# Quantised codes as smallest fp16 steps, scaled maxima on one engine, and a start without a barrier

## The reference

```python
def _fq(x, delta, zp, n_bits):
    xi = _round_ste(x / delta) + zp
    xq = jnp.clip(xi, 0.0, 2.0 ** n_bits - 1.0)
    return (xq - zp) * delta
...
sim = jnp.einsum('bhid,bhjd->bhij', _fq(q, dq, 128.0, 8), _fq(k, dk, 128.0, 8)) * SCALE
attn = jax.nn.softmax(sim, axis=-1)
out = jnp.einsum('bhij,bhjd->bhid', _fq(attn, dw, 0.0, 8), _fq(v, dv, 128.0, 8))
```

## Time and profile before

| | us |
|---|---|
| median of three runs (1578.14, 1579.74, 1579.89) | 1579.74 |
| the profiled execution | 1576.92 |
| its span in the trace | 1575.1 |
| VectorE busy | 1098.1 |
| PE busy | 1092.8 |
| ScalarE busy | 894.2 |
| GpSimd busy | 681.1 |

### The profile page before, as it was taken

The page is one execution under the profiler, slowest core; times in us unless marked ns, Lnnn a source line. Parts: engine busy times, 40 slices in busy tenths (PEclk is TensorE's granted clock), DMA queues, the critical chain, the costliest instruction groups (busy, mean ns, idle before and its releaser), DMA issues.

```text
span 1575.1 us, 28607 instructions
## 1 busy us (share of the span) xinstructions
PE 1092.8 (69%) x9344; PEld 593.3 (38%) x9344; DVE 1098.1 (70%) x3102; ACT 894.2 (57%) x2546; POOL 681.1 (43%) x1055
## 2 busy tenths in 40 slices
PE   2888888887788797855353545444358778888888
PEld 1333344444333286831120212222225435453545
DVE  2687777777688653678888999877765666666522
ACT  1555554555554464567676797988852344646531
POOL 3321011011011416558888888877741344445310
PEclk9899999999999998975555555555569799999989
DMA  5213142101331112267555576665530121201000
GB/s 184 61 53 92 51 129 75 54 24 50 99 106 49 42 39 82 57 160 122 99 104 109 106 130 115 121 109 106 109 57 14 27 48 35 49 21 43 1 0 27
DMA packets 265219, 116.53 MB, mean 74 GB/s; under 512 B 216936, under 2 KB 253936, under 8 KB 262896
## 3 DMA queue, kind: packets, MB, share of 16 engines
q1 hardware_dynamic: 260112, 108.29, 30.8%
q0 software_dynamic: 2048, 4.20, 0.9%
q10 hardware_dynamic: 2912, 2.22, 0.5%
HBM read 38.80 MB, written 16.45 MB: 35 GB/s over the span
## 4 chain that ended last, share of the span: by engine, by line
PE 35%; POOL 21%; DVE 18%; issue 14%; ACT 9%; DMA 1%; SPq 0%; POOLq 0%; another core or an unknown queue 0%; ACTq 0%; DVEq 0%
POOL arena L2289 12%; ACT arena L1581 4%; PE acc L1199 3%; POOL inv_total L2278 2%; PE trans L1171 2%; DVE minus_top L1980 2%; PE misc L1021 2%; PE misc L1027 2%; PE trans L1323 2%; ACT arena L1528 2%; PE score L1335 2%; PE score L1337 2%; PE trans L1177 1%; POOL arena L2235 1%; PE acc L1385 1%
## 5 line engine op out<-in xcount | busy, mean ns | idle before, releaser
L2289 POOL TENSOR_SCALAR arena<-arena,inv_total 128x512 f16<-128x512 f32 (+1 forms) x512 | 299.7, 585 | 57.3 <-DVE inv_total L2058 16.8
L1980 DVE TENSOR_REDUCE minus_top<-score 128x4 f32<-128x616 f32 (+4 forms) x256 | 200.6, 802 | 95.3 <-PE score L1141 36.9
L2154 POOL TENSOR_TENSOR rstd<-spread,minus_half 128x4 f32<-128x4 f32 x36 | 37.5, 1043 | 489.5 <-DVE spread L1662 414.0
L1581 ACT ACTIVATE arena<-score,minus_top,exp_scale 128x512 f32<-128x512 f32 (+1 forms) x340 | 210.4, 625 | 20.9 <-POOL arena L2289 11.9
L1528 ACT ACTIVATE arena<-trans 128x512 f32<-128x512 f32 x240 | 134.4, 596 | 109.3 <-PE trans L1177 104.0
L1619 ACT ACTIVATE arena<-arena,minus_top 128x154 f32<-128x154 f32 x256 | 105.2, 412 | 129.3 <-DVE minus_top L2123 129.1
L1280 PE MATMUL score<-arena 32*128 32x512 bf16 (+1 forms) x340 | 68.9, 458 | 139.7 <-ACT arena L1581 138.7
L2064 DVE TENSOR_REDUCE top_score<-score 128x2 f32<-128x1024 f32 (+1 forms) x128 | 135.7, 1061 | 0.6 <-PE score L1280 0.5
L2309 POOL TENSOR_TENSOR arena<-arena,inv_total 128x512 f32<-128x512 f32 x64 | 66.5, 1040 | 143.9 <-DVE inv_total L2131 130.0
L1581 ACT ACTIVATE arena<-trans,minus_top,exp_scale 128x154 f32<-128x154 f32 (+1 forms) x172 | 105.5, 620 | 19.2 <-POOL arena L2289 14.9
L2118 DVE CUSTOM_DVE_ANT_0 arena<-score,arena 128x154 f32<-128x154 f32 x256 | 65.9, 313 | 60.6 <-PE score L1360 60.2
(11 more groups left out here) (283 smaller groups left out, 2814.4 us busy)
## 6 DMA issues: line engine op xcount, KB each, us to landing
arena<-q_terms SPq DMA_DIRECT2D x88, 128.0 KB, 2.8
late<-arena SPq DMA_DIRECT2D x128, 64.0 KB, 2.0
q_terms<-arena SPq DMA_DIRECT2D x36, 128.0 KB
late<-k_terms SPq DMA_DIRECT2D x32, 128.0 KB, 3.1
arena<-arena SPq DMA_TRANSPOSE x192, 3.1
by_expert<-zeros SPq DMA_DIRECT2D x2, 1472.0 KB, 9.8
arena<-by_expert SPq DMA_DIRECT2D x10, 256.0 KB
from_expert<-arena SPq DMA_DIRECT2D x10, 256.0 KB
```

The costliest lines, as they stand in the source:

```text
L1581: ins = nc.scalar.activation(probs[:, i % 3, j, of], quant_score[i % 3][:, j, of], ACT.Exp, bias=minus_top[:, at_col:at_col + 1], scale=ex ...
L1980: nc.vector.tensor_reduce(dst, src, axis=AX.X, op=ALU.max, negate=True).then_inc(top_ready, 1)
L2289: ins = nc.gpsimd.tensor_scalar(codes[:, (i - 1) % CODE_SOURCES, j, to], probs[:, (i - 1) % 3, j, of], inv_total[:, at_col:at_col + 1], HA ...
```

## The change

- The codes are written as multiples of the smallest step of fp16, 2 ** -24: GpSimd multiplies by the reciprocal, which now has the step in it, and takes the minimum with 255 steps; the write itself rounds. The transposition goes straight to `pT_codes`, now fp16, the values are fp16 too, and the outputs are scaled by 2 ** 24 at L2072. `copy_codes` and its semaphore go; PE waits for the transposition.
- The maxima are scaled on VectorE, right behind the reduction, with a wait between the two; ScalarE's L1572 goes.
- VectorE's items in the quantised loop are taken from slot i - 1 at step i. The other engines' stay.
- The barrier behind the first loads goes. Loads, memsets and constants stand at the head of the engines' lists, and what needs them waits on new semaphores (`ident_in`, `first_weights_in`, `pads_in`, `pool_set`, `dve_set`). The first weights are the second load on SP; the eight late loads come after unit 0's reads. ScalarE copies one element early, which loads its table. Of the first eight reads of queries, ScalarE's queue issues four. The addition of a bias row to x of sequences 0 and 1 becomes an item "base" at slot 1.

The diff, cut to its core (moved memsets and the new waits inside items left out):

```diff
@@ -13,7 +13,7 @@
 ROUND = 1.5 * 2.0 ** 23
-HALF_ROUND = 1024.0
+CODE_STEP = 2.0 ** -24
 LOWEST = -1.0e30
@@ -21,7 +21,7 @@
 CODE_SOURCES = 4
-QUANT_LAG, WEIGH_LAG, GROUPED_LAG = 6, 8, 2
+WEIGH_LAG, GROUPED_LAG = 8, 2
 
@@ -217,7 +217,7 @@
                 at(exact, f, ("ctx", nxt))
-                at(exact, f + 1, ("x", nxt), ("pads", nxt))
+                at(exact, f + 1, ("x", nxt), ("pads", nxt), ("base", 0), ("base", 1))
             elif u + 1 < B:
@@ -554,13 +555,11 @@
 
-        v_quant, v_quant_tail = put([P, 2, TILES, HEADS, 32], bf16), put([P, 2, HEADS, 32], bf16)
+        v_quant, v_quant_tail = put([P, 2, TILES, HEADS, 32], fp16), put([P, 2, HEADS, 32], fp16)
         probs = put([P, 3, 2, TOKENS])
-        pT_at = quant_at[0]
-        pT_codes = put([P, CODE_SLOTS, 2 * TILES, P], bf16)
-        put = place(arena, [pT_at])
-        pT_raised = put([P, CODE_SLOTS, 2 * TILES, P], fp16)
+        pT_codes = put([P, CODE_SLOTS, 2 * TILES, P], fp16)
         put = place(arena, [0])
+
         codes = put([P, CODE_SOURCES, 2, TOKENS], fp16)
@@ -714,87 +717,27 @@
-        FIRST_SEQUENCE_LOADS, REST_LOADS = 4, 2
-
-        with nc.Block() as once:
-            loads = [(ident[:, :], io["ident"]), (sizes[:, :], io["sizes"].partition_broadcast(P)), (cols[:, :], io["cols"]),
-                     (term_row[:, :], io["term_row"]),
-                     (attn_w[:, 0:4, :], io["attn_w"][:, 0:4, :])]
-            late_loads = [(rows[:, :, :], io["rows"].partition_broadcast(P)), (norm_sel, io["norm_sel"]),
-                          (attn_w[:, 4:20, :], io["attn_w"][:, 4:20, :]), (expert_no[:, :], io["expert_no"]), (masks_f, io["masks"]),
...
+        FIRST_SEQUENCE_LOADS, PAD_LOADS, REST_LOADS = 2, 2, 2
+
+        loads = [(sizes[:, :], io["sizes"].partition_broadcast(P)), (cols[:, :], io["cols"]),
+                 (term_row[:, :], io["term_row"])]
...
+        POOL_SETS, DVE_SETS = 12, 27
+
+        with nc.Block() as block:
+
+            @block.sync
             def _(sp):
+                sp.dma_start(ident[:, :], io["ident"]).then_inc(ident_in, 16)
+                sp.dma_start(attn_w[:, 0:4, :], io["attn_w"][:, 0:4, :]).then_inc(first_weights_in, 16)
                 for dst, src in loads:
                     sp.dma_start(dst, src).then_inc(weights_in, 16)
-                for dst, src in late_loads:
-                    sp.dma_start(dst, src).then_inc(late_in, 16)
-
-            @once.scalar
-            def _(act):
-                for b, loaded in ((slice(0, 1), first_seq_in), (slice(1, B), rest_in)):
-                    act.dma_start(ctx_in[:, b, :, :], io["ctx"][:, b, :, :]).then_inc(loaded, 16)
-                    act.dma_start(x[:, b, :, :], x_dram[:, b, :, :]).then_inc(loaded, 16)
-                    if loaded is first_seq_in:
-                        act.dma_start(pad_rep.rearrange("p b k -> p (b k)"),
-                                      io["mask_BxS2_ff1"].rearrange("b k -> (b k)").partition_broadcast(P))\
-                            .then_inc(loaded, 16)
-                        act.dma_start(pad_col, io["pad_cols"]).then_inc(loaded, 16)
-
-            @once.gpsimd
-            def _(pool):
-                nc.gpsimd.memset(ones, 0.0).then_inc(cleared, 1)
-                nc.gpsimd.memset(ones_tail, 0.0).then_inc(cleared, 1)
-                nc.gpsimd.memset(ones_pad, 0.0).then_inc(cleared, 1)
-                nc.gpsimd.memset(v_tail, 0.0).then_inc(cleared, 1)
-                nc.gpsimd.memset(v_cols, 0.0).then_inc(v_cols_cleared, 1)
-                nc.gpsimd.memset(parts["k"][:, :, CTX:P + 32], 0.0)
-                nc.gpsimd.memset(ctxT_tail4[:, :, :, :], 0.0)
-                nc.gpsimd.memset(k_tail.rearrange("p a g k -> p (a g k)").bitcast(fp32), 0.0)
-                nc.gpsimd.memset(top_cols.rearrange("p a t j c -> p (a t j c)").bitcast(fp32), 0.0)
-                nc.gpsimd.memset(pad_rows, 0.0)
-                nc.gpsimd.memset(zeros[:, :], 0.0)
-                nc.gpsimd.memset(ones_bf[:, :], 1.0)
-                nc.gpsimd.memset(picked[:, :, :].rearrange("p t e -> p (t e)"), 0.0)
-                for i in range(2):
-                    nc.gpsimd.memset(blocks_to[i][:, 0:EXPERTS], 0.0)
-                pool.wait_ge(v_cols_cleared, 1)
-                wide = v_cols.rearrange("p t (a i j) c -> p (t a) i j c", i=2, j=4)
-                for i in range(2):
-                    nc.gpsimd.memset(wide[:, :, i, :, 16 + HD * i:16 + HD * (i + 1)], 1.0)
-
-            @once.vector
-            def _(dve):
-                dve.wait_ge(cleared, 4)
-                for j in range(4):
-                    at_row = 32 * top_place(j)
-                    nc.vector.memset(ones[at_row:at_row + 3, j, :], 1.0)
-                    nc.vector.memset(ones_tail[at_row:at_row + 3, 32 * j:32 * j + CTX_TAIL], 1.0)
-                for s in range(2):
-                    nc.vector.memset(ones_pad[s * STACK:s * STACK + 3, :], 1.0)
-                for j in range(4):
-                    rows_j = slice(32 * j, 32 * j + CTX_TAIL)
-                    for i in range(2):
-                        at_col = i * (P + HD) + 32 * j + 16
-                        nc.vector.memset(v_tail[rows_j, :, at_col:at_col + HD], 1.0)
-                nc.vector.memset(minus_half[:, :], -0.5)
-                dve.wait_ge(weights_in, 16 * len(loads))
-                nc.vector.tensor_copy(ident_bf[:, :], ident[:, :])
-                nc.vector.reciprocal(inv_sizes[:, :], sizes[:, :])
-                for n, name in enumerate(["L1_xattn_sa_bq", "L1_xattn_ca_bq"]):
-                    nc.vector.tensor_scalar(q_bias[:, n:n + 1], col(name), float(HD) ** -0.5, None, ALU.mult)
-                for n in range(2):
-                    q, k, vv, w = (sizes[:, 4 * n + i:4 * n + i + 1] for i in range(4))
-                    nc.vector.tensor_scalar(exp_scale[:, n:n + 1], q, k, float(HD) ** -0.5, ALU.mult, ALU.mult)
-                    nc.vector.tensor_scalar(out_scale[:, n:n + 1], vv, w, None, ALU.mult)
-        with nc.Block() as block:
-
-            @block.sync
-            def _(sp):
                 for u in EXACT_UNITS:
                     width = P + 32 if is_cross(u) else TOKENS
                     keys = (k_stack_ctx if is_cross(u) else k_stack)[:, u % 2, :, :]
@@ -834,9 +777,12 @@
-                        read_queries(slice(0, 2), q_first)
+                        read_queries(slice(0, 2), q_first, slice(0, PRODUCTS // 2))
                     read_queries(slice(0 if u else 2, PAIRS), q_stacked)
                     if u == 0:
+
+                        for dst, src in late_loads:
+                            sp.dma_start(dst, src).then_inc(late_in, 16)
@@ -923,7 +869,7 @@
-                    sp.dma_start_transpose(pT_raised[:, i % CODE_SLOTS, :, :],
+                    sp.dma_start_transpose(pT_codes[:, i % CODE_SLOTS, :, :],
@@ -1285,7 +1236,8 @@
-                    pe.wait_ge(codes_copied, 2 * n + 2)
+                    for i in (2 * n, 2 * n + 1):
+                        pe.wait_ge(codes_turned[i % CODE_SLOTS], 16 * (i // CODE_SLOTS + 1))
@@ -1342,7 +1294,6 @@
-                pe.wait_ge(codes_copied, len(QUANT_STEPS))
@@ -1506,11 +1459,25 @@
+                act.dma_start(ctx_in[:, 0:1, :, :], io["ctx"][:, 0:1, :, :]).then_inc(first_seq_in, 16)
+                act.dma_start(x[:, 0:1, :, :], x_dram[:, 0:1, :, :]).then_inc(first_seq_in, 16)
+                act.dma_start(pad_rep.rearrange("p b k -> p (b k)"),
+                              io["mask_BxS2_ff1"].rearrange("b k -> (b k)").partition_broadcast(P)).then_inc(pads_in, 16)
+                act.dma_start(pad_col, io["pad_cols"]).then_inc(pads_in, 16)
+
+                act.wait_ge(first_use_set, 1)
+                nc.scalar.copy(first_use[:, 1:2], first_use[:, 0:1])
+                act.dma_start(ctx_in[:, 1:B, :, :], io["ctx"][:, 1:B, :, :]).then_inc(rest_in, 16)
+                act.dma_start(x[:, 1:B, :, :], x_dram[:, 1:B, :, :]).then_inc(rest_in, 16)
                 for it in BEFORE[0]:
                     item(*it)
                 act.wait_ge(k_out, 48)
                 for n, term in enumerate(K_TERMS):
                     act.dma_start(k_stack_ctx[n::PRODUCTS, 0, :, :], k_terms_ctx.ap()[:, term, :, :]).then_inc(k_stacked, 16)
+                act.wait_ge(q_out, 48)
+                for n in range(PRODUCTS // 2, PRODUCTS):
+                    act.dma_start(q_stack[n::PRODUCTS, 0, 0:2, :], scratch["q"].ap()[:, Q_TERMS[n], 0:2, :]).then_inc(q_first, 16)
+                act.wait_ge(dve_set, DVE_SETS)
@@ -1569,11 +1536,8 @@
-                    nc.scalar.activation(of_step(minus_top, i), of_step(top_score, i), ACT.Copy,
-                                         scale=exp_scale[:, of:of + 1]).then_inc(quant_top_scaled, 1)
                     if i >= 3:
                         act.wait_ge(codes_ready, i - 2)
-                    act.wait_ge(quant_top_scaled, i + 1)
@@ -1993,6 +1959,31 @@
+                dve.wait_ge(cleared, 4)
+                for j in range(4):
...
```

(39 more changed lines are left out.)

78 lines of the change are left out of this document (67 added, 11 removed).

## The result

The changed kernel takes 1911.66 us (four runs, 1908.42 to 1913.85) against 1578.94 us before (four runs): a ratio of 1.2126, 95% interval 1.2100 to 1.2151. It is a fifth slower, and the prediction (1551, range 1534 to 1574) is wrong in size and in sign. The profiled execution took 1911.02 us, its span 1909.2.

What follows compares the result with a forecast made beforehand. GpSimd was taken to pace self attention 94 per cent of the time, and ScalarE, with GpSimd close behind, cross attention; savings of 7 + 10 + 10 + 0.4 = 27.4 us gave 1551 us, range 1534 to 1574.

Steps and rivals of the forecast that it cites:

- add becomes min: GpSimd's code instruction: add becoming min, and a second operation in the small multiplication, both cost nothing.
- Rival 4: GpSimd's code writes: numbers of a few smallest fp16 steps write slower, 54 ns each decides; far end 1684 us; chance 0.07.
- start, up to the first quantised reduction: Kernel start: VectorE gets K 5.1 us earlier, query reads save 2.5; -7 us taken, ends -3 and -8.
- self attention: Quantised self attention: GpSimd loses 5 of 7.5 us of slowing and 5 of 11.3 us of waits for VectorE, -10 us.
- cross attention: Quantised cross attention: 44 of 64 steps go from 2.23 us to GpSimd's 1.98 to 2.02, -10 us.
- after it: Tail: the last weighing no longer has a copy of 0.43 us before it, -0.4 us.
- the 290.5: Self attention on GpSimd without slowing or waits for VectorE: 128 steps of 1.95 us, gathers 20.9, small items about 20.
- rival 2: Both quantised parts: all slack opens and GpSimd runs at its bare pace, about 1533 us; chance 0.15.
- Small multiplication: VectorE's quantised steps: +0.35 us each, net -0.17 in self and 0 in cross; ends -0.3 and +0.35.
- Items a step later: Quantised loop: VectorE's items after the next reduction just fit, cost 0, other end +2 us per item.
- Rival 3: Item chains: the shift turns into stalls, 18 of about 1.1 us, 20 us, giving 1571 us; chance 0.16.
- The 3.65 us: Item-shift sum: VectorE begins the step 3.65 us after GpSimd's codes of step i-5 end, so W finishes at 7.3.

Runs made afterwards that it cites:

- e2: Changed kernel with GpSimd writing the codes as uint16 whole numbers, minimum with 255 kept: 1906.11 us, ratio 1.2107 to the kernel before.
- p1: Changed kernel with a code step of 1.0 instead of 2 ** -24, minimum kept, codes not rounded: 1916.25 us.
- p2: Changed kernel with codes, transposed codes and values in bf16 instead of fp16, minimum kept: 1915.02 us.
- e3: Changed kernel with addition of 0 in place of the minimum with 255 steps in GpSimd's code instruction: 1537.66 us, ratio 0.9751 to the kernel before.
- f2: f1 with 1024 added in place of 0 in the code instruction, nothing taking it away again, no copies: 1544.74 us.
- e5: e4 with the maxima scaled by ScalarE again instead of VectorE: 1538.01 us, ratio 0.9761 to the kernel before.
- e7: e1 with VectorE's items back at their own step: 1579.75 us, ratio 1.0017 to the kernel before.
- e1: Changed kernel with codes raised by 1024 and copied by VectorE as before: 1582.05 us, ratio 1.0029 to the kernel before.
- e4: e3 with VectorE's items back at their own step: 1536.10 us, ratio 0.9741 to the kernel before.
- e6: Kernel before with the new start alone: 1564.60 us, ratio 0.9924 to the kernel before.
- f1: e4 with codes in steps of 1 instead of 2 ** -24, not rounded: 1542.29 us.

## Why the prediction was wrong, step by step

**The step that failed** is in the paragraph on GpSimd: "add becomes min ... I cost both at nothing: the row for L2289 is the same shape and count of operations." Shape and count held; the kind of operation was the price, 1274 ns above the 721 of the earlier trace rows. No row of before has a minimum or a maximum on GpSimd: the minimum of the codes was in VectorE's copy. It was an operation that the trace doesn't show, and it needed a bound, which I gave to the small numbers and not to it. One row of group 3 did speak of it: L2154, a power of 4 columns, takes 1043 ns on this engine, while L2278, a product of 2 columns, takes 0.31 us. The two are different instructions as well, but they were a sign that the kind of arithmetic can have a price of its own on GpSimd, and I used that row only as a length.

**Rival 4** (chance 0.07) had the right place (this line) and the right sign, but a wrong mechanism (e2, p1 and p2 refute it; its sign came true by luck) and too small a price: +0.32 and +0.2 us at its far end, measured 1.27 and 0.36. Its way of deciding was sound: 54 ns an instruction turn the sign, and 1274 did.

**The rest of the sum** can be read from e3, which is the change with one word and its constant altered. Spans of the profiled executions, 1539.2 against 1575.1, are 35.9 less; 27.4 was forecast. But e3 adds 0, and the forecast priced every code by a row that adds 1024. f2 keeps that price (its items are at their own step): 11.0 us less than before in self attention (299.9) and 14.7 in cross attention (155.4).

| term | forecast | e3 against before |
|---|---|---|
| start, up to the first quantised reduction | -7 | -5.6 |
| self attention | -10 | -16.6 |
| cross attention | -10 | -13.9 |
| after it | -0.4 | +0.2 |

- Start: right in place and size. First scores at 24.6 to 25.2 (forecast 26), K at 9.9 (forecast 9.1); 8 us at the first scores, 4 to 8 at the first quantised reduction.
- Self attention: with f2's 11.0 the 10 was about right in size; e3's 16.6 has the addition of 0 in it. I let 5 of 7.5 us of slowing and 5 of 11.3 us of waiting go. Without copies and without the small multiplication (e5) it is 287.3, 23.6 less than before and below the 290.5 that I had built up from 1.95 us a step. "All slack opens" (rival 2) was nearer to e5, with an instruction that the forecast did not have.
- Small multiplication: "+0.35 per step ... VectorE is not the pacer, so by itself this is worth nothing except at its items" is wrong for self attention. The 0.2 to 0.35 us that I gave it hold about with copies (343 ns in e7, 364 in e1) and not without (445 in e3, 482 in e4); and it stands between a reduction and the exponential that waits for it, and costs 9.7 to 14 us (e4 against e5, e7 against e6). I had counted its time on VectorE's budget and not its delay on the path to ScalarE, and with it VectorE does set the pace of many steps (2.04 us in e7, 1.90 in e4). The ends of that term don't come out either: 0.13 + 0.17 - 0.52 is -0.22 and not -0.3, and 0.13 + 0.69 - 0.52 is +0.30 and not +0.35.
- Cross attention: mis-sized, 13.9 or 14.7 for 10. GpSimd's pace of 1.98 to 2.02 came from the earlier trace rows, which has copies beside it and adds 1024. Without copies it is 1.91 (f2, four codes of 0.48), so most of that pace was the instruction's own. With 0 added, 12 codes, three steps, take 4.54 us, 1.51 each, and ScalarE's 1.82 sets the pace (e4). Outside the clusters that gives 0.4 a step, not 0.23.
- Items a step later: costed at 0, end +2 us an item. Measured: -2.7 in self and +5.1 in cross, no difference in the median (e3, e4). Rival 3's 20 us are not there. The 3.65 us in that paragraph's sum stand in no row shown.

GpSimd's timeline in cross attention without copies and with 0 added (e4), against the earlier trace rows:

```profile
1045.13 4.54 POOL L2295 TENSOR_SCALAR arena<-arena,inv_total 128x154 f16<-128x154 f32 x12
```

## What to carry to other kernels

An instruction on the engine that sets the pace is priced by its kind of operation too, not by shape and count alone: if no row of that engine shows the operation, it has no price yet, and one word can be worth more than the rest of a change. When something small is moved to an engine with time to spare, look at who waits for the result and not only at the engine's busy time. Where two stages have different full engines, the same small work may belong on a different engine in each, and the stage times of a few variants show it before the medians do.

## What the runs showed of the hardware

- GpSimd's TENSOR_SCALAR with a minimum or maximum takes 1995 to 2020 ns at 128x512 against 695 to 702 for product and addition of 0, and 810 to 832 ns at 128x154 against 400 to 404, the minimum in either place; with the minimum second it is so for fp16, bf16 and uint16 output. The two widths give an estimate of 3.3 ns a column, (1995 - 811) / 358, against 0.8, (702 - 404) / 358. The Trainium skill ("GPSIMD Engine Reference", § 4.1 Engine selection) puts elementwise add, mul and max in one row and calls operations with one input roughly line-rate on GpSimd; for product and addition nothing here speaks against it, for the maximum the measurement does, and it decides.
- Writing numbers of a few smallest fp16 steps costs GpSimd nothing: 695 ns (e4), and 695 with steps of 1 (f1).
- Adding 1024 in place of 0 costs 0.10 us an instruction from start to start, at 512 columns as at 154; a calm step is 1.91 us in place of 1.69 (f2, f1). The size of what is written changes with it.
- VectorE's small multiplication is stretched while GpSimd adds, and only in a part of the time in which it takes a minimum. VectorE's timeline, f2 (adds), then two moments of the changed kernel, the first with GpSimd's instructions beside it:

```profile
685.11 0.67 DVE L2049 TENSOR_SCALAR minus_top<-top_score,exp_scale 128x2 f32<-128x2 f32 x1
...
709.05 3.97 POOL L2295 TENSOR_SCALAR arena<-arena,inv_total 128x512 f16<-128x512 f32 x2
...
710.47 0.61 DVE L2049 TENSOR_SCALAR minus_top<-top_score,exp_scale 128x2 f32<-128x2 f32 x1
...
716.10 0.23 DVE L2049 TENSOR_SCALAR minus_top<-top_score,exp_scale 128x2 f32<-128x2 f32 x1
```

GpSimd has a code instruction under way at all three moments, as its timelines show (685.06 for 1.46 us; 709.05 for 3.97; 713.47 for 3.96). The Trainium skill ("SBUF — State Buffer", § Who interferes with whom) has VectorE's tensor_scalar in a two-port mode and GpSimd exclude each other for a whole instruction. f2 agrees: its 0.67 us end at 685.78, where the first of the two code instructions ends (685.06 and half of 1.46), and in e4 82 of the 88 multiplications of self attention that began within an addition were stretched and ended with it. The minimum does not agree, and the measurement decides: of 123 that began within one, 96 took 0.23 to 0.25 us, nearly all of them begun 0.50 to 0.66 us after it. The 7 begun in its first 0.33 us ended 0.70 us after its start, and the 20 begun between 1.39 and 1.50 us after its start ended with it, as the one at 710.47 does. Why a minimum lets VectorE through in its middle I did not test.
